# Moving two raw boxes, the first centred boxes and two copies around the statistics of a windowed-ratio kernel

## The reference

```
v     = group norm of x, 32 groups of 6 channels, mean and variance over (rows, w, 6 channels), eps 1e-5
s     = box_sum(v, w, 5)                      # sliding sum of 5 along w, zero padded
num   = box_sum(s * s, c, 20)                 # sliding sum of 20 along c
d     = box_sum(box_sum(v * v, w, 5), c, 20)
norm  = box_sum(ones over w, 5)               # 5 inside, 3 or 4 at the edges
out   = x + nan_to_num(num / (d * norm), nan=1)
```

## Time and profile before

| | us |
|---|---|
| median of 3 runs | 383.45 |
| lowest, highest | 383.27, 388.59 |
| the profiled execution, its own time | 388.08 |
| span of the profiled execution | 386.4 |
| mean granted TensorE clock in it | 0.979 of full |
| TensorE busy | 362.7 (94%) |
| DVE, ACT, POOL busy | 296.8, 273.7, 249.7 |

### The profile page before, as it was taken

How to read it: one execution, slowest core, us unless ns; L and a number is a source line. 1 busy time by engine, 2 the same in 40 slices (tenths; PEclk the granted TensorE clock), 3 DMA queues, 4 the chain that set the end, 5 groups by cost and what they waited for, 6 DMA issues and landing times.

```text
span 386.4 us, 7863 instructions
## 1 busy us (share of the span) xinstructions
PE 362.7 (94%) x2976; PEld 356.9 (92%) x2976; DVE 296.8 (77%) x608; ACT 273.7 (71%) x384; POOL 249.7 (65%) x168
## 2 busy tenths in 40 slices
PE   1999988999999999999779999999999999999982
PEld 1999988999999999999779999999999999999981
DVE  2999963566679999999953777778887777777774
ACT  1555549998999999987633777777777777777751
POOL 4000053888788888887165788777778777777631
PEclk9999989999999999999986999999999999999998
DMA  8999200578898963222202121122222222222114
GB/s 238 327 328 328 86 2 0 165 240 252 273 289 279 286 217 129 83 84 83 81 0 83 52 79 58 61 81 83 81 83 83 82 83 84 81 85 76 59 60 135
DMA packets 66486, 50.84 MB, mean 132 GB/s; under 512 B 912, under 2 KB 66448, under 8 KB 66448
## 3 DMA queue, kind: packets, MB, share of 16 engines
q1 hardware_dynamic: 66448, 50.34, 42.2%
HBM read 25.17 MB, written 25.17 MB: 130 GB/s over the span
## 4 chain that ended last, share of the span: by engine, by line
PE 82%; DVE 9%; ACT 4%; DMA 2%; issue 2%; POOL 1%; DVEq 0%; POOLq 0%; ACTq 0%
PE N L520 21%; PE S L511 17%; PE U L511 17%; PE D L520 14%; PE N L511 5%; PE S L520 4%; DVE late_triples L660 3%; PE D L561 3%; DMA xs<-x 2%; DVE ratio L768 2%; DVE N L771 2%; ACT xs L446 1%; PE U L604 1%; ACT q L464 1%; DVE ratio L777 1%
## 5 line engine op out<-in xcount | busy, mean ns | idle before, releaser
L354 POOL TENSOR_TENSOR xs<-xs,ratio 128x768 f32<-128x768 f32 x63 | 114.7, 1820 | 65.8 <-DVE ratio L777 65.8
L348 POOL TENSOR_TENSOR xc<-xs,mean_c 128x768 f32<-128x768 f32 x64 | 117.3, 1834 | 47.5 <-DVE mean_c L669 45.5
L768 DVE SCALAR_TENSOR_TENSOR ratio<-D,q 128x768 f32<-128x768 f32 x51 | 48.5, 952 | 48.5 <-ACT q L470 48.5
L771 DVE SCALAR_TENSOR_TENSOR N<-N,q 128x768 f32<-128x768 f32 x64 | 61.5, 960 | 8.5 <-PE N L520 6.4
L777 DVE SCALAR_TENSOR_TENSOR ratio<-ratio,N 128x768 f32<-128x768 f32 x64 | 61.1, 954 | 6.7 <-DVE N L771 0.5
L464 ACT ACTIVATE q<-D 128x768 f32<-128x768 f32 x51 | 41.3, 810 | 29.1 <-PE D L520 19.3
L470 ACT ACTIVATE q<-q 128x768 f32<-128x768 f32 x64 | 54.0, 844 | 2.0
L511 PE MATMUL S<-b,xc 128*128 128x128 f32 x432 | 55.1, 278 | 0.0
L437 ACT ACTIVATE xs<-S 128x768 f32<-128x768 f32 x36 | 29.2, 811 | 35.5 <-PE S L511 35.5
L520 PE MATMUL N<-b_r,xs 128*128 128x138 f32 (+2 forms) x384 | 53.6, 289 | 0.0
L511 PEld LDWEIGHTS S<-b,xc 128*128 128x128 f32 x432 | 52.4, 195 | 0.0
(11 more groups left out here) (87 smaller groups left out, 458.6 us busy)
## 6 DMA issues: line engine op xcount, KB each, us to landing
out<-xs SPq DMA_DIRECT2D x31, 768.0 KB, 3.8
xs<-x SPq DMA_DIRECT2D x8, 1536.0 KB, 15.0
xs<-x SPq DMA_DIRECT2D x16, 768.0 KB, 5.8
out<-xs SPq DMA_DIRECT2D x2, 384.0 KB, 2.6
```

The lines of the kernel that those rows point to most:

```text
L348: nc.gpsimd.tensor_tensor(pairs(xc[:, n % XC_RING, :]), pairs(x_flat(n)), mean, ALU.subtract)\
L354: nc.gpsimd.tensor_tensor(x_flat(n), x_flat(n), ratio[:, n % RATIO_RING, :], ALU.add)\
L768: nc.vector.scalar_tensor_tensor(t1, in_bank(d_bank(n)), -TINY, pairs(q[:, n % Q_RING, :]), ALU.add, ALU.mult).then_inc(t1_ready, 1)
L771: nc.vector.scalar_tensor_tensor(in_bank(N), in_bank(N), TINY, pairs(q[:, n % Q_RING, :]), ALU.add, ALU.mult).then_inc(t2_ready, 1)
```

## The change

- `FIRST_FILL` = 26: TensorE does 26 raw boxes, then the three remaining block averages (5, 6, 7), and only then raw boxes 26 and 27. Box 26 goes to bank U, box 27 to bank S (`raw_bank`), and the waits for a free bank follow from that (`raw_bank_free`).
- The warm matmuls (`keep_warm`, `WARM`) are gone. TensorE does `box_u(0)` ahead of `average_squares(0)`; `box_u(0)` also waits until raw box 26 is copied out of bank U.
- ACT copies raw box 26 ahead of the square of the deviations and raw box 27 after `square_xc(0)`. It copies `u(0)` ahead of the bands instead of after them, and does `square_xc(2)` ahead of `square_raw(0)`. It no longer copies `u(1)`.
- DVE copies `u(1)` between the first and the second part of `mend_edges`.
- The second moments' sum moves from bank S to bank D, the spread offsets from bank S to bank N. So `sum_n(0)` (bank N) now waits for both parts of `mend_edges`, and `sum_d(1)` (bank S) for the raw copies instead.

```
+FIRST_FILL = RAW_DUOS - 2
-WARM = 8
-        m2_sum = [S[:, 0, 0:GROUPS], ...]
-        offsets_wide_ps = S[:, 1, 0:CHUNKS * 128]...
+        m2_sum = [D[:, 0, CHUNKS * 128:CHUNKS * 128 + GROUPS], ...]
+        offsets_wide_ps = N[:, 1, 0:CHUNKS * 128]...
+        def raw_bank(n):
+            if n < FIRST_FILL:
+                return (S, N)[n % 2]
+            return (U, S)[n - FIRST_FILL]
+        def raw_bank_free(n):
+            return max([k + 1 for k in range(n) if raw_bank(k) is raw_bank(n)], default=0)
 # ACT
-            for n in range(RAW_DUOS):
+            for n in range(FIRST_FILL + 1):
                 keep_raw(n)
             act.wait_ge(dev_ready, 1)
             nc.scalar.activation(dev[0], dev[0], ACT.Square).then_inc(dev_squared, 1)
             square_xc(0)
+            keep_raw(FIRST_FILL + 1)
             square_xc(1)
+            keep_u(0)
             act.wait_ge(inv_ready, 1)
             (the bands)
-            keep_u(0)
+            square_xc(2)
             square_raw(0)
-            keep_u(1)
-            square_xc(2)
 # TensorE: box_u(0)
+                else:
+                    pe.wait_ge(raw_kept, FIRST_FILL + 1)
 # TensorE: sum_d(1), then sum_n(0)
-                    pe.wait_ge(edges_ready, 2)
+                    pe.wait_ge(raw_kept, RAW_DUOS)
-                    pe.wait_ge(raw_kept, RAW_DUOS)
+                    pe.wait_ge(edges_ready, 2)
 # TensorE, order
-            for n in range(RAW_DUOS):
+            for n in range(FIRST_FILL):
                 box_raw(n)
                 ...
-            average_block(LOADS - 2)
-            average_block(LOADS - 1).then_inc(mean_in_psum, 1)
-            pe.wait_ge(raw_kept, RAW_DUOS)
+            for j in range(FIRST_FILL // LOAD_DUOS - 1, LOADS):
+                mm = average_block(j)
+            mm.then_inc(mean_in_psum, 1)
+            for n in range(FIRST_FILL, RAW_DUOS):
+                box_raw(n)
+            pe.wait_ge(raw_kept, FIRST_FILL)
             pe.wait_ge(mean_ready, 1)
             spread_offsets().then_inc(offsets_in_psum, 1)
-            keep_warm()
+            box_u(0)
             average_squares(0).then_inc(var_in_psum, 1)
-            box_u(0)
             box_u(1)
 # DVE
-            dve.wait_ge(raw_kept, RAW_DUOS)
+            dve.wait_ge(raw_kept, FIRST_FILL)
             ...
             mend_edges(0, STEP_DUOS)
+            dve.wait_ge(u_ready, 2)
+            nc.vector.tensor_copy(pairs(u[:, 1, :]), in_bank(U)).then_inc(us_ready, 1)
+            dve.wait_ge(raw_kept, RAW_DUOS)
             mend_edges(STEP_DUOS, RAW_DUOS - STEP_DUOS)
```

More of the change, by code:

```diff
@@ L131, in window_ratio_kernel @@
                beside[0].rearrange("p (g t) -> p g t", g=GROUPS)]
-        m2_sum = [S[:, 0, 0:GROUPS], beside[1][:, 2 * GROUPS:3 * GROUPS]]
-        offsets_wide_ps = S[:, 1, 0:CHUNKS * 128].rearrange("p (j w) -> p j w", j=CHUNKS)
+        m2_sum = [D[:, 0, CHUNKS * 128:CHUNKS * 128 + GROUPS], beside[1][:, 2 * GROUPS:3 * GROUPS]]
+        offsets_wide_ps = N[:, 1, 0:CHUNKS * 128].rearrange("p (j w) -> p j w", j=CHUNKS)
         offsets_ps = offsets_wide_ps[:, :, 0:COEFS]
@@ L399, in keep_raw @@
             def keep_raw(n):
-                bank = (S, N)[n % 2]
                 act.wait_ge(raw_in_psum, n + 1)
-                nc.scalar.activation(pairs(raw_box(n)), in_bank(bank), ACT.Copy).then_inc(raw_kept, 1)
+                nc.scalar.activation(pairs(raw_box(n)), in_bank(raw_bank(n)), ACT.Copy).then_inc(raw_kept, 1)
             def square_xc(n):
@@ L528, in box_raw @@
                     pe.wait_ge(loaded0[n // LOAD_DUOS], 16)
-                if n >= 2:
-                    pe.wait_ge(raw_kept, n - 1)
-                box5((S, N)[n % 2], x_flat(n), b5).then_inc(raw_in_psum, 1)
+                if raw_bank_free(n):
+                    pe.wait_ge(raw_kept, raw_bank_free(n))
+                box5(raw_bank(n), x_flat(n), b5).then_inc(raw_in_psum, 1)
             def box_s(n):
@@ L599, in average_squares @@
                 return mm
-            def keep_warm():
-                for _ in range(WARM):
-                    nc.tensor.matmul(U[:, 0, 0:W], b5[:, :], b5d[:, :], start=True, stop=True)
             def spread_offsets():
```

## The result

The changed kernel takes 382.48 us in the median of 22 runs (381.14 to 385.79); the kernel before, now over 22 runs, 385.13 (quickest 383.23; one run of 544.06 is so far outside all others that nothing here rests on it). The medians differ by 2.65 us; the ratio is 0.9937, 95% interval 0.9916 to 0.9957, or about 2.4 us quicker. The interval leaves out 1, but the change is within the 2% called no change. The forecast of 381.0 is the time of the six quickest runs (381.14 to 381.31), not of the median. The profiled execution took 381.17, its span 379.5 with a clock of 0.998 [before: 386.4 and 0.979].

A forecast was written before the change was run, and what follows sets the result against it. TensorE was taken as four fifths of the chain, with ACT 93% busy. Its 3.1 us lead, cut to 2.5 by ACT at duo 4, took 383.45 to 380.95, rounded 381.0; range 380.2 to 386.5.

The forecast's parts named there:

- The order of work: Opening to duo 4: boxes 26 and 27 cover DVE's and POOL's work; ACT gets 1.95 us ahead, TensorE 3.1.
- of 3.1 us 2.5 are left at duo 4: At `box_u(4)` ACT binds: its lead of about 2.1 plus 0.45 slack leaves TensorE 2.5 us ahead, kept afterwards.
- 0.33 was forecast: Opening: with two fewer boxes ahead of it, the mean's reduction starts at 50.25 in place of 50.58.
- The gain of 0.33 is lost: ACT's square of the deviations queues behind the copy of box 26, starting at 52.35 against 52.26; `ssq_c` 54.3 against 54.23.
- the prediction's own sum: Opening: `square_xc(0)` starts at 53.16 against 53.49, ends at 54.00; `box_u(0)` then takes TensorE from 54.05 to 55.39.
- DVE's copy: DVE's copy of `u(1)` takes 0.97 us from 58.16, leaving 0.28 to spare ahead of `box_u(2)`; at 1.42 it costs 0.17.
- `box_u(0)` first, warm matmuls gone: Opening: variance matmuls at full clock, 0.67 us for 1.04; variance's fold and ACT's bands each come 0.67 us earlier.
- rival 1: Opening: half clock for one 3.4 us stretch from about 49.6; the lead is about 1.0, time 382.4; chance 0.14.
- They cost nothing as long as the clock is full: Opening: raw boxes 26 and 27, moved behind the mean, cover DVE's and POOL's work, costing nothing at full clock.
- The level of the median: Whole kernel: the median before, 383.45, was taken as without the late half-clock stretch; less 2.5 gives 380.95, rounded 381.0.
- Rival 3: Join of the batches: the median run has the late half-clock stretch, so 385.6 to 386.1; chance 0.32.

The follow-up runs named there:

- run 11: The kernel before, its opening unchanged, with fifteen unread matmuls in the two idle times at the join: median 383.24 us, quickest 383.08, ratio to before 0.9967.
- run 10: The changed kernel with the join's idle times filled and ACT's square of the deviations ahead of its copy of raw box 26: quickest 381.01 us.
- run 9: The changed kernel with the join's idle times filled and DVE's copy of `u(1)` done twice: median 381.12 us (381.03 to 381.29).
- run 4: The changed kernel with `u(1)` copied by ACT behind the bands instead of by DVE: quickest 382.11 us, median 382.47.
- run 1: The kernel before with its eight warm matmuls taken out, nothing else changed: median 385.37 us, quickest 384.58, ratio 1.0037.
- run 5: The changed kernel with variance matmuls ahead of `box_u(0)` and bands ahead of the copy of `u(0)` again: quickest 381.33 us, median 382.27.
- run 6: The changed kernel itself measured again on a second chip: median 381.62 us (381.08 to 382.83), profiled execution 382.83.
- run 8: The changed kernel with `u(2)` copied by DVE as well: quickest 380.58 us, median 381.76, profiled execution 382.11.
- run 2: The changed kernel with all 28 raw boxes ahead of the mean, warm matmuls still gone: median 384.50 us, quickest 383.10, ratio to before 1.0004.
- run 3: As run 2, plus twelve unread matmuls, four ahead of the mean's wait and eight ahead of `box_u(0)`: quickest 381.72 us, median 382.69, ratio to before 0.9959.
- run 7: The changed kernel with fifteen unread matmuls in TensorE's two idle times at the join: median 381.08 us (380.98 to 381.35), ratio to before 0.9905.
- run 12: The changed kernel with DVE copying `u(2)`, six unread matmuls ahead of the last block average and fifteen at the join: median 380.39 us, ratio to before 0.9897.

## Why the prediction was right, and where not

**The order of work: right.** DVE's statistics hold the mean, the two boxes fill TensorE's wait, and ACT and not TensorE sets the lead. Forecast was that of 3.1 us 2.5 are left at duo 4; the rows give 3.2 at `box_u(3)`, 2.84 at `box_u(4)` (70.97 to 68.13) and 2.5 from `box_u(5)` on (75.20 to 72.68), so ACT binds a duo longer. The lead at the join is 2.47 and, with the join equal, 2.2 in the medians. Part of the difference is the traces. Counted from the mean's reduction, `box_u(32)` starts 149.80 us behind it before and 149.79 in run 11, and 147.92 in the changed kernel: 1.9 us are gained there. The rest is the mean, and its gain isn't a constant: 50.01 to 50.93 in the five traces with all 28 boxes ahead of it, 49.87 to 50.43 in the nine with 26, on average 0.5 us earlier, where 0.33 was forecast. The kernel before's profiled execution had its mean at 50.58 and run 11's at 50.01; that the first pair of traces gave 2.47 is partly luck.

**"The gain of 0.33 is lost" behind the copy of box 26: lost, but not on the path.** `ssq_c` is ready 3.96 us behind the mean's reduction (53.95) against 3.65 before, so the copy does cost it 0.3. But TensorE was in `box_u(0)` until 55.4, and run 10, which moved the square ahead of the copy, gained nothing. The early mean reaches the end by the other way, POOL's centring and `square_xc(0)` (52.92 against 53.49), from which the prediction's own sum starts `box_u(0)`.

**DVE's copy: the price was right, the cover understated.** 0.96 us, where 0.97 was taken. Its cover is the 0.3 in front of `box_u(2)` and TensorE's lead over ACT behind it: a second copy, 0.67 us late at `box_u(2)`, is 0.06 late at `box_u(5)` (run 9). Giving it to DVE is worth 1.0 us (run 4), more than ACT's 0.8.

**`box_u(0)` first, warm matmuls gone** was counted as 0.67 us on the bands. The fold did come 0.71 earlier, but by another sum: 0.59 of it is the earlier mean. Behind the mean's reduction the fold stands at 6.36 us before and 6.24 in the changed kernel. Taking out the warm matmuls brings it forward (5.47 in run 1, though at half clock, and 5.09 in run 5), and `box_u(0)` ahead of it takes nearly all of that back. It does no harm, because the fold is not what is late (run 5).

**The clock: seen, but on the wrong side of the account.** I set the half clock of the new idle time as rival 1 at 1.4 us; it exists (runs 6 and 8) and costs 1.0 us in run 6 (the first root 11.16 us behind the mean's reduction against 10.16). What I missed is that the boxes behind the mean take the warm matmuls' place: both profiled executions with neither (runs 1 and 2) have 10.2 and 6.7 us at half clock in the opening. Of the 2.0 us between run 2 and the changed kernel at the quickest, 1.4 are this (run 3). Run 2, with everything of the change but the boxes' move, is no quicker than the kernel before (383.10 against 382.93 on that chip), so at half clock the rest of the change shows nothing. "They cost nothing as long as the clock is full" was an account of half of it: they also keep it full, as twelve unread matmuls would.

**The level of the median** was the term that was off by 1.5 us. I took the median of three runs, 383.45, as the kernel without half clock at the join. Over 22 runs it is 385.13: most runs have some. The changed kernel's median is 1.5 above the forecast for the same reason, and that the medians still differ by about the 2.5 forecast is in part luck: both levels were off by nearly the same (1.7 and 1.5 us). Rival 3 had the mechanism, with only two sizes (none, or 4.9 us); the profiled executions show more. A stretch from 193.1 to 196.5 falls in front of the wait at `box_u(32)`, which hides much of it: from the late mean's matmul to `box_u(32)` there are 7.35 us at full clock (190.56 to 197.91), and 7.58, 7.78 and 8.85 with it (runs 4, 6 and 2), so 0.2, 0.4 and 1.5 us. It costs 3.1 where it falls from 199 to 206 (384.46 in run 5 against 381.33), and 4.4 to 4.6 from 199.9 to 210.1.

**Open:** in run 11 executions with a mean clock of 0.997 and of 0.993 take the same 383.2, and only the profiled one (383.08, 0.993) shows where its half clock lay (52 to 55.5 us). What the opening's half clock costs the kernel before itself isn't settled by this, and so neither is how much of the 2.2 us is the clock. Nor is it known why its middle group at 385 is so narrow.

## What to carry to other kernels

Useful work that can wait is the better warm matmul: look for it before deleting or adding unread ones, and test the deletion with the clock's row, not with busy time. When an engine's queue binds (here ACT's), price each edit on that queue: a variance 1.2 us earlier brought nothing (run 5), and one 0.8 us copy moved to an idle engine 1.0 (run 4). Before comparing two traces to a tenth of a microsecond, count from an event behind the data's arrival: here the mean's reduction moved by up to 0.9 us between traces of kernels with the same work ahead of it. Where times fall into groups, find the idle time in front of each half-clock stretch before trusting a median of three; fifteen unread matmuls at the join took 1.8 us off the median of the kernel before (385.01 to 383.24, same chip) and left its quickest run at 383.08.

## What the hardware showed that I had not expected

The same idle time (1.9 us at 189 to 193, 2.7 us ahead of `box_u(32)`) brings half clock in some executions and none in others. In the opening the longer idle time isn't even the worse one: half clock followed 1.87 and 1.94 us of idleness ahead of the last block average (runs 6 and 8), and none followed 2.13 and 2.16 us (runs 5 and 7). The half-clock stretches lasted between 3.4 and 10.2 us though TensorE worked in them. The Trainium skill, "TensorE: Matmul & The Clock Gate", section "Part 1: The HAM clock gate", says that the monitor runs freely and doesn't start with the kernel; the groups of times are in line with it, though no run here shows the monitor itself. With unread matmuls in both idle times, none of the profiled executions of experiments 7, 9, 10, 11 and 12 has half clock at the join, though 0.89 us of idleness are left there in that of 7.
